# Round 1's outputs copied in place of added to cleared rows, the first square added sooner, routing's end spread over round 1, and the last splits moved in both halves

## The reference

```python
xn = _layernorm(x)
# attention: 32 heads of 128, decayed causal scores within 256 tokens
qkv = silu(xn @ qkv_w.T); gate = sigmoid(xn @ gate_w.T)
attn = decayed_causal_scores(q, k) @ v            # per head
xf = attn * rsqrt(mean(attn * attn, over 4096) + EPS)
a = (gate * norm_w * xf) @ out_w.T
# experts: groups of 4, 2 groups kept, 2 of 16 experts per token
scores = softmax(xn @ router_w + router_b) + router_bias
idx, gate_e = top2(masked_by_group(scores))
y = sum_e gate_e * ((silu(xn @ w1 + b1) * (xn @ w2 + b2)) @ w3 + b3)
z = (silu(xn @ sw1 + sb1) * (xn @ sw2 + sb2)) @ sw3 + sb3
x = x + a + y + z                                 # then layer 1
```

## Time and profile before

| what | value |
|---|---|
| median of 3 runs | 2642.59 us (2640.86 to 2643.15) |
| profiled execution, device time | 2645.89 us |
| its span | 2644.0 us |
| PE busy | 2536.7 us, 96% |
| VectorE, ScalarE, GpSimd busy | 1118.6, 1090.9, 1359.3 us |

### The profile page before, as it was taken

The page is one execution under the profiler, slowest core; times in us unless marked ns, Lnnn a source line. Parts: engine busy times, 40 slices in busy tenths (PEclk is TensorE's granted clock), DMA queues, the critical chain, the costliest instruction groups (busy, mean ns, idle before and its releaser), DMA issues.

```text
span 2644.0 us, 40129 instructions
## 1 busy us (share of the span) xinstructions
PE 2536.7 (96%) x13674; PEld 2181.6 (83%) x13674; DVE 1118.6 (42%) x1903; ACT 1090.9 (41%) x2031; POOL 1359.3 (51%) x1357
## 2 busy tenths in 40 slices
PE   7999999999999999879999999999999988969999
PEld 5788888888888888768888888888888877857777
DVE  6333333333333334763333333333333478864453
ACT  4443434444434443433434344344344347733332
POOL 5655555555555552765555555555555368831110
PEclk9999999999999999999999999999999999989999
DMA  4211111111111112211111111111111079821100
GB/s 152 94 46 53 46 46 46 61 46 46 52 54 46 46 46 70 99 47 54 46 53 46 46 46 61 46 46 52 54 46 46 21 253 322 273 92 48 33 32 32
DMA packets 73151, 187.81 MB, mean 71 GB/s; under 512 B 12098, under 2 KB 15826, under 8 KB 73094
## 3 DMA queue, kind: packets, MB, share of 16 engines
q1 hardware_dynamic: 64550, 170.26, 18.8%
q0 software_dynamic: 8544, 16.82, 2.3%
HBM read 168.13 MB, written 26.79 MB: 74 GB/s over the span
## 4 chain that ended last, share of the span: by engine, by line
PE 83%; DVE 7%; ACT 3%; DMA 3%; issue 2%; POOL 2%; ACTq 0%; POOLq 0%; SPq 0%; DVEq 0%
PE bank L88 23%; PE bank L89 23%; PE bank L90 23%; PE bank L931 4%; PE bank L917 4%; PE bank L933 2%; PE bank L918 2%; DMA exin<-xn_rows,ecur 2%; DVE el L1992 1%; ACT exth L1951 1%; ACT eh L1960 0%; ACT eh L1956 0%; DMA l_stage<-y_slots,slot_of 0%; POOL l_stage L2496 0%; DVE ebias L1991 0%
## 5 line engine op out<-in xcount | busy, mean ns | idle before, releaser
L88 PE MATMUL bank<-xh,wh 128*128 128x512 f32 x1400 | 558.9, 399 | 3.3 <-ACT bank L1132 1.8
L90 PE MATMUL bank<-xh,wl 128*128 128x512 f32 x1400 | 545.7, 390 | 0.0
L1603 POOL TENSOR_TENSOR wl<-raw,wh 128x512 fp32r<-128x512 f32 x196 | 251.2, 1297 | 165.8 <-ACT wh L1177 163.3
L1425 DVE TENSOR_TENSOR acc<-bank,acc 128x512 f32<-128x512 f32 x256 | 176.9, 691 | 339.7 <-PE bank L90 339.7
L89 PE MATMUL bank<-xl_sums,wh 128*128 128x512 f32 x800 | 315.5, 394 | 0.0
L88 PEld LDWEIGHTS bank<-xh,wh 128*128 128x128 f32 x1400 | 263.2, 188 | 56.9 <-ACT bank L1132 2.3
L90 PEld LDWEIGHTS bank<-xh,wl 128*128 128x128 f32 x1400 | 262.8, 188 | 56.9
L88 PE MATMUL bank<-wh,xh 128*128 128x256 f32 x1024 | 293.9, 287 | 4.1 <-DVE xl L476 3.4
L1388 DVE TENSOR_TENSOR ms<-bank,dcur 128x384 f32<-128x384 f32 x256 | 142.4, 557 | 354.9 <-PE bank L918 345.7
L90 PE MATMUL bank<-wh,xl 128*128 128x256 f32 x1024 | 291.4, 285 | 0.0
L89 PE MATMUL bank<-wl,xh 128*128 128x256 f32 x1024 | 291.2, 284 | 0.0
(11 more groups left out here) (335 smaller groups left out, 5326.3 us busy)
## 6 DMA issues: line engine op xcount, KB each, us to landing
raw<-in_w_pairs_dram SPq DMA_DIRECT2D x128, 512.0 KB, 3.9
raw<-in_o_pairs_dram SPq DMA_DIRECT2D x32, 512.0 KB, 3.1
eraw<-in_ex_dram SPq DMA_DIRECT2D x31, 513.0 KB
y_slots<-ey SPq DMA_DIRECT2D x31, 512.0 KB
dcur<-in_decay_dram SPq DMA_DIRECT2D x32, 384.0 KB, 2.9
eraw<-in_ex_dram SPq DMA_DIRECT2D x31, 256.0 KB
l_raw<-in_l_w_dram SPq DMA_DIRECT2D x28, 192.0 KB
out_dram<-acc SPq DMA_DIRECT2D x16, 256.0 KB, 2.1
```

The costliest lines, as they stand in the source:

```text
L88: pe.matmul(out, wh, mh, start=start and i == 0, stop=False, skip_group_check=True)
L90: ins = pe.matmul(out, wl, mh, start=False, stop=stop and i == n - 1, skip_group_check=True)
L1425: v.tensor_tensor(now[:, t, :], op[t % 2][:], now[:, t, :], ALU.add).then_inc(v_acc, 1)
L1603: pool.tensor_tensor(wl[:, cols], src, wh[:, cols].bitcast(F32), ALU.subtract).then_inc(w_lo, 1)
```

## The change

1. The clearing of `far` is gone, with its semaphore. `add_out` of unit 0 copies the bank into `now`. In the second half the copies of tiles 2 and up wait for `v_gates`, since these tiles hold routing's tables.
2. Round 1 is written out on ScalarE, VectorE and GpSimd in both halves (`two_first`). Round 0's section 2 and V splits, and their low parts, move from the end of round 0 into round 1 (before, only ScalarE's in the second half stood there). GpSimd adds the first square before V's low parts and the next weight addition.
3. Routing: PE does product 2 of section 2 before the two counting matmuls. `place` moves from the end of round 0 into round 1, behind the second low part of y. `gates_and_experts` is cut in two, `gates_of_choices` before the first output copy and `experts_of_tiles` after the second. GpSimd waits for both and sends the first slots behind the low parts of section 1.
4. In the second half's round 0, the scores 0 and 1 come before V projections 2 and 3.
5. At the end of the first half the hidden shared rows' low parts of the second group go behind the second `finish`, the first two `refill.low` go between the two shared products, the mean is taken before the last output add, and ScalarE makes six in place of four high parts before the hidden ones.

```diff
@@ -253,13 +253,14 @@
-def gates_and_experts(self, v, gate_of, expert_of, gates, ready):
+def gates_of_choices(self, v, gate_of):
     c = self.chain
...
+def experts_of_tiles(self, v, expert_of, gates, ready):
+    c = self.chain
     c.link(v.tensor_copy(self.red, self.ends))
@@ -986,14 +988,14 @@
     section(n, 1, *ORDER)
-    section(n, 2, *ORDER[:3])
+    section(n, 2, *ORDER[:4])
     if last:
...
                   stop=True).then_inc(pe_pre, 1)
-    section(n, 2, *ORDER[3:])
+    section(n, 2, *ORDER[4:])
 else:
@@ -1045,12 +1047,19 @@
+if zero(n) and last:
+    scores(n, 0)
+    scores(n, 1)
+    project_v(n, 2)
+    project_v(n, 3)
+    return
 for i in range(3):
...
 scores(n, 1)
-if last or not zero(n):
+if not zero(n):
     project_v(n, 3)
@@ -1198,7 +1207,7 @@
 first = zero(n)
-second = last and isinstance(n, int) and n == 1
+second = isinstance(n, int) and n == 1
 if first:
@@ -1328,20 +1337,21 @@
         take(n, 2, "b")
+    if first:
+        for i in range(4):
+            if last and i not in early:
+                take_v(n, i)
+        return
     for i in range(4):
-        if not (first and last):
-            if more:
-                split(n, 2, i)
-        elif i in early:
-            continue
-        if last or not first:
-            take_v(n, i)
-    if more and not (first and last):
+        if more:
+            split(n, 2, i)
+        take_v(n, i)
+    if more:
         for i in range(2):
...
-(two_first if last else all_rounds)(a, run)
+two_first(a, run)
@@ -1361,10 +1371,10 @@
     return
-for i in range(4):
+for i in range(6):
     refill.high(a, i)
 hidden_high(0)
-for i in range(4, 8):
+for i in range(6, 8):
     refill.high(a, i)
@@ -1420,8 +1430,14 @@
 wait(v, pe_out, 8 * u + t + 1)
-if t == 0:
-    wait(v, p_zero, 1)
+if zero(u):
+    if t == 0 and not last:
+        v.wait_ge(dma_xn, 16 * NT)
+    if t == 2 and last:
+        v.wait_ge(v_gates, 1)
+    v.tensor_copy(now[:, t, :], op[t % 2][:]).then_inc(v_acc, 1)
+    return
 v.tensor_tensor(now[:, t, :], op[t % 2][:], now[:, t, :], ALU.add).then_inc(v_acc, 1)
@@ -1441,6 +1457,10 @@
+def mean_square():
+    wait(v, pe_sums, 1)
+    v.tensor_scalar(mean, ot[:, 0:HTILES], 1.0 / (H * DH), EPS, ALU.mult, ALU.add).then_inc(v_var2, 1)
 def low_shared(g, i):
@@ -1486,12 +1507,12 @@
 summed(n, 0, "e")
-if last and isinstance(n, int) and n == 1:
-    router.gates_and_experts(v, gate_of, expert_of, gates, v_gates)
 gated(u, 1)
...
 y_low(u, 1)
+if second and last:
+    router.place(v, slot_of, v_slots)
 if end:
@@ -1502,9 +1523,13 @@
                     ALU.subtract).then_inc(v_b3, 1)
+if second and last:
+    router.gates_of_choices(v, gate_of)
 add_out(u, 0)
...
 add_out(u, 1)
+if second and last:
+    router.experts_of_tiles(v, expert_of, gates, v_gates)
 add_out(u, 2)
@@ -1519,11 +1544,16 @@
 shared_product(1, 1)
+if not last:
+    refill.low(v, 0)
+    refill.low(v, 1)
 shared_product(1, 0)
...
     if not last:
-        for i in ((0, 1), (2, 3), (4, 5), (6, 7))[t - TPG]:
+        for i in ((), (2, 3), (4, 5), (6, 7))[t - TPG]:
             refill.low(v, i)
+        if t == HTILES - 1:
+            mean_square()
     add_out(u, t)
@@ -1538,24 +1568,19 @@
     mask(n, 1)
-    if first and last:
-        router.place(v, slot_of, v_slots)
-(two_first if last else all_rounds)(v, run)
+two_first(v, run)
...
             low_shared(g, i)
+    mean_square()
 else:
-    for i in range(2):
-        low_shared(1, i)
     refill.low(v, 8)
...
 c = Chain(v, v_chain, 5 * h)
-wait(v, pe_sums, 1)
-v.tensor_scalar(mean, ot[:, 0:HTILES], 1.0 / (H * DH), EPS, ALU.mult, ALU.add).then_inc(v_var2, 1)
 rsqrt(v, a_root2, 1 + h, c, mean, root, rs)
@@ -1582,6 +1607,9 @@
 finish(t)
+if t == 1 and not last:
+    for i in range(2):
+        low_shared(1, i)
 if last:
@@ -1658,31 +1686,47 @@
 shared = isinstance(n, int) and n == UNITS - 1
-if sends:
+second = isinstance(n, int) and n == 1
+if second:
+    section_low(0, 2)
+    add_squares(0, 0)
+    plain_low(wh[:, V_AT:WALL], wl[:, V_AT:WALL], split_at(0, "v"))
+if sends and not second:
     pick(u, 0 if shared else n)
 add(n, 0, 16 * (3 * n + 2))
-if sends:
+if sends and not second:
     send(0)
 if not first:
-    add_squares(u, 0)
+    if not second:
+        add_squares(u, 0)
     add_squares(u, 1)
 section_low(n, 0)
-if sends:
+if sends and not second:
     pool.wait_ge(ids_out, 32 * u + 16)
...
     add_squares(u, 2)
-if sends:
+if sends and not second:
     send(1)
...
 if sends:
-    sent(u)
+    if second:
+        pool.wait_ge(v_slots, 2)
+        pool.wait_ge(v_gates, 1)
+        pick(u, n)
+        send(0)
+    else:
+        sent(u)
     if shared:
...
 plain_low(oh, ol, split_at(n, "o"))
+if sends and second:
+    pool.wait_ge(ids_out, 32 * u + 16)
+    send(1)
 if sends and shared:
@@ -1691,20 +1735,18 @@
 add(n, 2, 16 * (2 * n + 3))
+if first:
+    if last:
+        pool.wait_ge(dma_z, 16)
+        pool.wait_ge(dma_ids, 16)
+        pool.tensor_scalar(tok_ids, tok_ids, -T, None, ALU.add).then_inc(p_ids, 1)
+        pool.wait_ge(p_ids, 1)
+    return
 section_low(n, 2)
 plain_low(wh[:, V_AT:WALL], wl[:, V_AT:WALL], split_at(n, "v"))
-if first:
-    if last:
-        wait(pool, v_gates, 1)
-        pool.wait_ge(v_slots, 2)
-        pool.wait_ge(dma_z, 16)
-        pool.wait_ge(dma_ids, 16)
-        pool.tensor_scalar(tok_ids, tok_ids, -T, None, ALU.add).then_inc(p_ids, 1)
-        pool.wait_ge(p_ids, 1)
-    else:
-        wait(pool, dma_xn, 16 * NT)
-    pool.memset(far, 0.0).then_inc(p_zero, 1)
+if sends and second:
+    sent(u)
@@ -1733,7 +1775,7 @@
 section_low(None, 2)
-all_rounds(pool, run)
+two_first(pool, run)
 if last:
```

More of the change, by code:

```diff
@@ L273, in gates_and_experts @@
         v.tensor_tensor(gates[:, :, 0:E], self.lg, self.sc, ALU.mult).then_inc(ready, 1)
+        v.wait_ge(ready, 1)
 A11, A12, S1, A22, S3, S2, S4 = range(7)
@@ L303 @@
          "a_yh": 68, "a_root2": 1, "w_hi": 266, "w_lo": 266, "v_c": 100, "v_mask": 128, "v_y": 64, "v_yl": 68, "v_acc": 128,
-         "v_sh": 4, "v_var2": 1, "v_fin": 8, "x_fin": 8, "v_nw": 16, "p_comb": 200, "p_sq": 65, "p_zero": 1,
+         "v_sh": 4, "v_var2": 1, "v_fin": 8, "x_fin": 8, "v_nw": 16, "p_comb": 200, "p_sq": 65,
          "dma_r0": 16 * 50, "dma_r1": 16 * 33, "dma_d": 256, "dma_again0": 64, "dma_again1": 64}
@@ L572, in attention @@
                              "v_nw"))
-        p_comb, p_sq, p_zero, x_fin, w_lo = (sem(n) for n in ("p_comb", "p_sq", "p_zero", "x_fin", "w_lo"))
+        p_comb, p_sq, x_fin, w_lo = (sem(n) for n in ("p_comb", "p_sq", "x_fin", "w_lo"))
         blocks = [Blocks(0, ps[3:8], [gT[:, 0, :], early_sums[0][:], gT[:, 1, :], early_sums[1][:]]),
@@ L1693, in run @@
                     add(n, 2, 16 * (2 * n + 3))
-                    section_low(n, 2)
-                    plain_low(wh[:, V_AT:WALL], wl[:, V_AT:WALL], split_at(n, "v"))
                     if first:
                         if last:
-                            wait(pool, v_gates, 1)
-                            pool.wait_ge(v_slots, 2)
                             pool.wait_ge(dma_z, 16)
@@ L1704, in run @@
                             pool.wait_ge(p_ids, 1)
-                        else:
-                            wait(pool, dma_xn, 16 * NT)
-                        pool.memset(far, 0.0).then_inc(p_zero, 1)
+                        return
+                    section_low(n, 2)
+                    plain_low(wh[:, V_AT:WALL], wl[:, V_AT:WALL], split_at(n, "v"))
+                    if sends and second:
+                        sent(u)
                 def pick(m, t):
```

## The result

| | before | changed |
|---|---|---|
| median, same chip | 2642.87 us (2640.86 to 2645.16, 4 runs) | 2622.12 us (2620.79 to 2623.11, 4 runs) |
| profiled execution, its span | 2645.89, 2644.0 us | 2621.40, 2619.4 us |

That is 20.8 us less by the medians, 24.5 less by the two profiled executions.

A forecast was written before the change was run, and what follows sets the result against it. The prediction took PE to bound the kernel, with gains in what PE waits in four places: 6.3 + 2.0 + 2.3 + 13.2 = 23.8 us off 2642.6, say 2619 us. Own range 2615 to 2623, with R1, R2 and R3 2612 to 2628.

The forecast's parts named there:

- A: Round 1 of the first half: the wait on the square goes, 0.7 us of new wait; gain 6.3 us (5 to 7).
- B: End of the first half: low parts moved, transpose wait goes, root steps held by GpSimd's sum; gain 2.0 us (0 to 4).
- C: Round 0 of the second half: shorter masks' wait, gate tile wait filled by scores; gain 2.3 us (1.4 to 2.8).
- D: Round 1 of the second half: 15.06 us lost, less 1.9 of new waits; gain 13.2 us (9 to 14.6).
- R: Start of round 1, from which the forecast counted its events; the first half's second square was to be done at R + 14.7.
- they stand until 1066.0: First half's end: VectorE's root steps wait for GpSimd's last sum, so finish 0 comes at about 1067.5 instead of 1069.86.
- its sum for product 4 is ready about when PE asks: Second half's round 1: VectorE's sum, behind experts, two copies and a low part, costs PE a new wait of 0.3 us.
- likeliest case: The main forecast for the whole kernel, 2619 us, own range 2615 to 2623, chance 0.66.
- R1: Rival: routing becomes the bound of round 1, new waits 6 us and B at 0; time 2625, chance 0.11.
- R2: Rival: the square stays late, parts 5 us later, each half gives back 3.5; time 2626, chance 0.07.
- R3: Rival: all covers hold, B is 4, new waits 0.5 and none in A; time 2615, chance 0.12.
- R4: Rival: lateness passes to loop rounds, 1 us a round gives 2647; chance 0.04 together with unknown mishaps.

The follow-up runs named there:

- sums_cut: The changed kernel with GpSimd's last sum of 1024 columns at the first half's end made in four operations of 256 columns; 2620.74 us, ratio 0.9914.
- t5_first: The changed kernel with ScalarE taking t5 of section 1 ahead of its splits in round 1; 2621.26 us, ratio 0.9904.
- best2: The changed kernel with t5 ahead of the splits, two masks inside count, place before the second low part, product 4's sum amid the expert table; 2615.28 us.
- sq_late: The changed kernel with GpSimd's first square addition put back behind V's low parts and the weight additions, both halves; 2644.9 us, ratio 0.9994.
- copy_only: The kernel before with unit 0's outputs copied and the clearing gone, all orders kept; 2643.44 us beside 2646.59, ratio 0.9992.
- again: The changed kernel unaltered, timed a second time; 2622.2 us beside 2645.78 for the kernel before, ratio 0.991.

## Why the prediction was right, and where it was off

The sum stands at 23.8 forecast and 23.67 measured in the stretches, but two of its terms are off, B by 1.65 us too little and D by 1.8 too much. That they cancel is luck.

| part | forecast | measured | from |
|---|---|---|---|
| A | 6.3 | 6.40 | 65.83 - 59.43 |
| B | 2.0 | 3.65 | 939.74 - 936.09 |
| C | 2.3 | 2.24 | 52.31 - 51.07, and 1.00 of masks' wait that D was charged |
| D | 13.2 | 11.38 | 76.83 - 64.45, less that 1.00 |

**A was right**, the new order of events too: the addition at 92.9, the second square at 95.22 (forecast R + 14.1 with R = 81.13), t5 late, 0.21 us of wait at the copied output (0.5 forecast).

**B was under-sized.** The mechanism was as forecast: the root stands until GpSimd's last sum ends (one step of it, 2.18 us), and the transposes' wait goes. The step that failed is "they stand until 1066.0": less the 5.54 us by which the mark moved that is 1060.5, and the sum ended at 1059.7. Two causes make these 0.73 us. GpSimd's sum was itself stretched before beside VectorE's low parts (2.68 us, now 2.36). And it began 0.41 sooner, counted from the mark, since the transposes that GpSimd's sums wait for came sooner: PE's wait on their low parts is the one that fell from 1.2 to 0.5, which the forecast of B left out. Finish 0 then came at 1060.91, 3.4 earlier than before counted from the mark (1069.86 - 5.54 = 1064.32), where my own chain had 2.4 and I took 2.0; the root's steps behind the sum took 1.2 us where I had 1.5, and another 0.24 us lies behind finish 0. sums_cut shows that the hold is real, so 2 was the right end to choose for that reason; the measured size is near the other end, 4, for the reasons just given.

**C was right**: 0.75 us of masks' wait left, no gate tile wait.

**D was over-sized**: "the sum is 1.9 us of new waits". They were 1.00 (masks, 0.45 forecast), 0.64 (copied output, 1.15 forecast) and 1.39 (sum for product 4, 0.3 forecast), 3.0 together and with restarts 3.7 (15.06 - 11.38). The step that failed is "its sum for product 4 is ready about when PE asks": I had the experts at 3.5 to 4 us, and they took 4.7 (a copy of 16 columns stood from 1151.37 to 1152.68, beside one GpSimd operation that ended at 1152.65; no run tests this hold), behind a sum "c" for which ScalarE's t5 was late by another 1.24. t5_first and best2 show both causes: 0.8 and 1.7 us.

**The time**: 2619.0 forecast, 2622.12 measured, inside the likeliest case's own range. The working gave 2622.1 for a profiled execution that had 2645.89; I then took the gain from the median shown, 2642.59. The 3 us between forecast and result are this step: later medians of before (2644.9 to 2646.6) lie nearer the profiled execution than that first one, and beside 2645.78 the changed kernel was 23.6 us faster.

**The rivals.** R1 is refuted: routing's waits came to 3, not 6. R2 is refuted by 1137.79, the square without a wait, and priced by sq_late: had the addition stayed behind the load, all 24 us would have gone, where I had priced a lateness of 5 us at 7. R3 had B nearly right and fell on D's new waits. R4 is refuted: ScalarE's idle time at the late weight addition (6.59 us in the first half, 6.63 in the second) is made up within the round: PE has no wait from 109 us to the first half's end at 1045, and B, which holds 14 loop rounds, is shorter.

## What to carry to other kernels

When two engines meet in a ring of queues, look for the one instruction that releases the wait and ask what stands ahead of it: moving a 1.3 us addition ahead of a load's consumers was worth 24 us, and taking 3.5 us of work from the same queue twice, without it, nothing that the medians show. Price what you push to a later place by its duration and by every instruction queued behind it, since the tail that moved (a table of 4.7 us) became the next wait. And cut traces at marks on the bound engine: differences of 0.5 us stand out there which five timed runs do not resolve.

## What the runs showed that I had not expected

An operation of 8 columns on VectorE (two inputs) took 2.18 us beside a GpSimd operation of 2.36 us (2.17 to 2.19 in the nine profiles that have this end with the sum in one piece), and 0.66 at most beside four short ones; the four cost GpSimd 2.80 in place of 2.36.

A wait of the same length did not always cost PE its clock. The stretch behind the first half's wait on the square, window, length, busy times and clock, in the kernel before (a wait of 2.94 us) and in copy_only (3.00 us):

```profile
102.00:106.00 4.00, 4.00 (x15) 3.42 (x15) 2.25 (x3) 3.42 (x7) 2.56 (x3) 0.58 0.00 0
```

```profile
102.00:106.00 4.00, 3.33 (x19) 3.05 (x20) 2.71 (x4) 3.97 (x8) 1.94 (x2) 1.00 0.00 0
```

The first restarts at 1.2 GHz (0.58 of full speed on average), the second at 2.4. That is 1.6 us of A between two kernels with the same waits there, so 1.6 of the 7.03 us which the forecast counted in A may belong to that execution and not to the kernel. That one kernel can do both is shown by its two profiles. Finish 0 ended a wait of PE in each, in the changed kernel and in again:

```profile
1061.72 0.80 PE L88 MATMUL bank<-wh 128*128 128x512 f32 x1 [2.44 <-DVE acc L1590]
```

```profile
1062.74 0.50 PE L88 MATMUL bank<-wh 128*128 128x512 f32 x1 [2.43 <-DVE acc L1590]
```

In the 6 us that followed the granted clock was 0.74 in the first and 1.00 in the second. It cost nothing here: in again PE reached finish 2 early and waited 1.08 us for it, and B is the same (936.09 and 936.12). After waits of 9 to 11 us the lower level followed each time (two values of 256 columns took 1.22 us, where they take 0.69 to 0.70 at full speed).
